# Layer 1 of a two-layer convolution kernel: r and kernel matmuls one product later, the rest of the kernel split in PSUM, VectorE's rest step behind product 8

## What is computed

```python
r = einsum('oc,bchw->bohw', w_reduce, x) + b_reduce
rn = relu(batch_norm(r))
kern = einsum('kc,bchw->bkhw', w_span, rn) + b_span      # 9 values for each pixel
z = softplus(einsum('bkhw,bckhw->bchw', kern, patches))  # 9 shifted copies of x, times kern, summed
y = softplus(conv3x3(z, w_conv2) + b_conv2)
x = x + y
```

## Time and profile before

| | |
|---|---|
| Time, median of 3 runs | 10453.66 us (10447.23 to 10459.92) |
| The profiled execution's own time | 10458.6 us |
| Its span | 10456.8 us |
| Mean granted TensorE clock | 0.971 of full speed |
| PE / DVE / ACT / POOL busy | 91% / 59% / 64% / 47% of the span |
| Layer 1's loop, from about 7619 us | 132 strips, the last product ends at 10443.4 us |

### The profile page before, as it was taken

The page is one execution under the profiler, slowest core; times in us unless marked ns, Lnnn a source line. Parts: engine busy times, 40 slices in busy tenths (PEclk is TensorE's granted clock), DMA queues, the critical chain, the costliest instruction groups (busy, mean ns, idle before and its releaser), DMA issues. The chain is left out here.

```text
span 10456.8 us, 157100 instructions
## 1 busy us (share of the span) xinstructions
PE 9479.5 (91%) x52698; PEld 5411.0 (52%) x52698; DVE 6192.1 (59%) x7749; ACT 6664.2 (64%) x9055; POOL 4891.7 (47%) x2751
## 2 busy tenths in 40 slices
PE   0399999999999999999999999998878888888888
PEld 0266666666666666666666666665222222222222
DVE  4455555555555555555555555555668878888887
ACT  0277676677776776776677777774056666666666
POOL 0233333333333333333333333332067777777777
PEclk9999999999999999999999999999989999999998
DMA  9511111111111111111111111113933333333333
GB/s 195 110 46 45 45 45 45 45 45 45 44 41 42 45 45 45 45 45 45 45 45 45 45 42 40 44 45 80 213 90 95 92 94 94 95 94 92 93 93 95
DMA packets 614703, 715.13 MB, mean 68 GB/s; under 512 B 42861, under 2 KB 576803, under 8 KB 593807
## 3 DMA queue, kind: packets, MB, share of 16 engines
q1 hardware_dynamic: 614670, 714.73, 29.1%
HBM read 549.68 MB, written 164.89 MB: 68 GB/s over the span
## 5 line engine op out<-in xcount | busy, mean ns | idle before, releaser
L507 PE MATMUL banks<-w_hi,hi_lo 128*128 128x256 f16 x18432 | 2351.3, 273 | 53.3 <-DVE hi_lo L731 53.3
L507 PEld LDWEIGHTS banks<-w_hi,hi_lo 128*128 128x128 f16 x18432 | 1784.4, 98 | 458.3 <-ACT qk L622 206.1
L465 POOL TENSOR_TENSOR u_im<-q_im,k_swap 128x512 f32<-128x512 f32 x512 | 701.6, 1370 | 2438.4 <-ACT q_im L640 2402.7
L1161 POOL TENSOR_TENSOR part_sum<-part_sum,prod 128x1024 f32<-128x1024 f32 x660 | 1558.6, 2362 | 53.8 <-DVE prod L1438 1.0
L1196 PE MATMUL banks<-z,conv_w 128*128 128x512 f32 x3136 | 1542.8, 629 | 0.0
L740 DVE TENSOR_TENSOR u<-q_re,banks 128x512 f32<-128x512 f32 x512 | 351.2, 686 | 1893.0 <-ACT q_re L645 1477.4
L622 ACT ACTIVATE qk<-banks,inv_wscale 128x512 f32<-128x512 f32 x1024 | 690.5, 687 | 1069.9 <-PE banks L507 1056.9
L468 POOL TENSOR_TENSOR u<-u,u_im 128x512 f32<-128x512 f32 x512 | 650.6, 1271 | 934.1 <-DVE u L740 934.1
L524 PE MATMUL banks<-hi_lo,w_hi 128*128 128x512 f16 x4608 | 1080.6, 380 | 0.0
L507 PE MATMUL banks<-w_lo_pair,hi_pair 128*128 128x256 f16 x6144 | 1006.1, 273 | 0.0
L455 POOL TENSOR_TENSOR hl_all<-xn,hi_all 64x1280 f16<-64x1280 f32 x258 | 793.9, 3077 | 272.2 <-ACT hi_all L615 260.1
(11 more groups left out here) (191 smaller groups left out, 17316.0 us busy)
## 6 DMA issues: line engine op xcount, KB each, us to landing
xr<-in_x_dram SPq DMA_DIRECT2D x258, 640.0 KB, 8.2
xb<-y_scratch SPq DMA_DIRECT2D x268, 320.0 KB, 4.8
xa<-y_scratch SPq DMA_DIRECT2D x270, 256.0 KB, 5.3
x_res<-in_x_dram SPq DMA_DIRECT2D x258, 256.0 KB, 4.1
out_dram<-res SPq DMA_DIRECT2D x258, 256.0 KB, 5.0
xc<-in_x_dram SPq DMA_DIRECT2D x64, 1024.0 KB, 12.9
y_scratch<-ys SPq DMA_DIRECT2D x256, 256.0 KB, 4.1
yc<-y_scratch SPq DMA_DIRECT2D x256, 256.0 KB, 5.6
```

The costliest lines, as they stand in the source:

```text
L465: nc.gpsimd.tensor_tensor(u_im[:], q_im[:], k_swap[:], ALU.mult).then_inc(u_made, 1)
L507: r = pe.matmul(out, px, w, start=n == 0, stop=n == 13)
L1161: nc.gpsimd.tensor_tensor(part_sum[:], prod[0][:] if n == 0 else part_sum[:], prod[n + 1][:], ALU.add)\
```

## The change

Three things, all in layer 1. On TensorE, the first half of r stands behind select 4 (was 3), the second half behind select 5 (was 4), and the kernel rows behind select 7 (was 6). `k_rest` is no longer a tile of SBUF; it is the columns 256 to 511 of bank 7. Since bank 7 then holds data that `third_parts` still reads, TensorE's waits for `rest_made` become waits for `third_made`, one of them in every strip in front of half 1 of the convolution. On VectorE, `rest` stands behind product 8 (was between 6 and 7), ahead of the sum that follows product 8.

```diff
-            k_rest = tsb("k_rest", [P, 256])
...
+            k_rest = bank[7][:, 256:512]
...
                             select(n, k, 9 * k + n)
                             if n == 1 and any_2:
                                 conv(b, 1, (4, 5))
-                            if n == 3:
+                            if n == 4:
                                 pe.wait_ge(mid_normed, i * 4 + (k + 3))
                                 if any_2:
                                     pe.wait_ge(resid_added[1], i * 4 + (k - 1))
                                 else:
-                                    pe.wait_ge(rest_made, i * 4 + (k + 2))
+                                    pe.wait_ge(third_made, i * 4 + (k + 2))
                                 r_product((k + 2) % 4, 0)
-                            if n == 4:
+                            if n == 5:
                                 pe.wait_ge(rn_ready, i * 8 + (2 * k + 5))
                                 r_product((k + 2) % 4, 1)
-                            if n == 6:
+                            if n == 7:
                                 pe.wait_ge(rn_ready, i * 8 + (2 * k + 6))
                                 weights()
...
                         select(0, (k + 1) % 4, 9 * k + 9)
                         if any_1:
-                            pe.wait_ge(rest_made, i * 4 + (k + 3))
+                            pe.wait_ge(third_made, i * 4 + (k + 3))
                             conv(1 - b, 1, (0, 1))
...
-                            if n == 6:
+                            if n == 8:
                                 rest(i * 4 + (k + 2))
                         v.wait_ge(prod_ready, i * 36 + (9 * k + 9))
                         add_to_x(prod[8])
                         third_parts(i * 4 + (k + 2))
```

More of the change, by code:

```diff
@@ L1244, in _ @@
                     if u:
-                        pe.wait_ge(rest_made, u)
+                        pe.wait_ge(third_made, u)
                     r_product(u, 0)
@@ L1322, in second_parts @@
                     act.wait_ge(rest_made, u + 1)
-                    act.copy(k_parts[:, 1, :], k_rest[:]).then_inc(second_made, 1)
+                    act.copy(k_parts[:, 1, :], k_rest).then_inc(second_made, 1)
                 def conv_abs(v, b, h, ring_used):
@@ L1403, in rest @@
                         v.wait_ge(third_made, u + 0)
-                    v.scalar_tensor_tensor(k_rest[:], b_r[:, 0:256], span_b[:, 0:1], k_parts[:, 0, :], ALU.add, ALU.subtract)\
+                    v.scalar_tensor_tensor(k_rest, b_r[:, 0:256], span_b[:, 0:1], k_parts[:, 0, :], ALU.add, ALU.subtract)\
                         .then_inc(rest_made, 1)
@@ L1408, in third_parts @@
                     v.wait_ge(second_made, u + 1)
-                    v.tensor_tensor(k_parts[:, 2, :], k_rest[:], k_parts[:, 1, :], ALU.subtract).then_inc(third_made, 1)
+                    v.tensor_tensor(k_parts[:, 2, :], k_rest, k_parts[:, 1, :], ALU.subtract).then_inc(third_made, 1)
                 def residual(i, k, age, h):
```

## The result

The changed kernel takes 10287.1 us (median of four, 10281.47 to 10289.03) against 10453.69 for the kernel before: 0.984 of it, 95% interval 0.9823 to 0.9857, or 166.6 us less. The forecast was 10324 with a range from 10288, so the sign was right and the gain came, as forecast, with fewer stretches of TensorE's low clock; the size was not right: 36.9 us more came than forecast, 0.9 us beyond the range.

What follows compares the result with a forecast made beforehand. A waiting loop through several engines set the 21.43 us strip, with TensorE's slow clock adding 1.2 to 1.3. Full-clock 20.2 plus 0.25 gave 20.45: 1.0 us over 130 strips, 130 us less, 10324 against the median; range 10288 to 10460.

Steps and rivals of the forecast that it cites:

- Two loops, P and X: Layer 1: P is TensorE's residual, r, kernel rows and convolution; X is `third_parts`, store, fetches, load of `xb`, `x_up`.
- Select 4 and 5 ahead of r: TensorE, before r: select 4 runs in the 1.85 us idle piece, r undelayed; product 5 ends at 8569.15 instead of 8569.86.
- Kernel rows behind select 7: TensorE, before the convolution: select 7 waits for product 5 either way, so a gain of 0.1 us at most.
- rest behind product 8: VectorE: `rest` adds 0.41 us ahead of the sum and `third_parts`; ScalarE's second part fits beneath the sum.
- k_rest in PSUM: VectorE: `third_parts` becomes constant, taken as 0.48 us, with bounds 0.41 and the mean of about 1.5.
- The new wait: TensorE before convolution half 1 waits for `third_parts`: 0.15 us later than before, giving about 20.2 us a strip.
- ScalarE's later chain: ScalarE behind the later `rest`: residual half 0 and product 0 about 0.95 us later, some 0.7 us of cover remaining.
- Rival 4: ScalarE's later chain binds: perhaps 20.8 us a strip, -80 us, 10374; counted within the forecast's case (0.56).
- The clock: TensorE's shorter idle pieces leave a 1.66 us slow stretch in one strip of six: 20.2 + 0.25 = 20.45 us.
- Rival 1: TensorE's clock falls as often as now: strip 21.25 to 21.45 us, time 10445 (10425 to 10465); chance 0.24.
- rival 3: More slow stretches on TensorE, one of 1.66 us in every strip: 21.86 us, +56 us, 10510; chance 0.10.
- Rival 2: `third_parts` keeps its 1.49 us mean and TensorE waits before convolution half 1: +130 us, 10584; chance 0.10.

Runs made afterwards that it cites:

- PSUM alone: The kernel before with `k_rest` in bank 7 and waits for `third_made` instead of `rest_made`, nothing moved: 10367.5 us.
- filling: The kernel before with four extra selection matmuls ahead of select 3, in TensorE's idle piece before r: 10415.4 us.
- the two runs with `rest` earlier: The changed kernel with `rest` behind product 6 (10271.1 us) or behind product 7 (10264.0 us), all else as changed.
- PSUM with eight matmuls: The kernel before with `k_rest` in PSUM and eight extra selection matmuls ahead of select 3, old order: 10308.7 us.
- the three PSUM kernels with the old order: The kernel before with `k_rest` in PSUM and no, four or eight extra matmuls ahead of select 3: 10367.5, 10335.2, 10308.7 us.
- the order alone: The kernel before with only TensorE's new order (r behind select 4 and 5, kernel rows behind select 7): 10269.6 us.

## Why the prediction was right in its direction and short in its size

- *What bounds the strip.* Two loops, P and X, with slow stretches on the first: right. But the whole excess of 1.25 us over a strip at full clock was put down to the clock. PSUM alone removes 0.74 us of it and leaves 0.63 slow stretches of about 1.3 us; filling takes away nearly half of the stretches and gives 0.24. At 1.3 us for each, the 0.79 stretches of before are 1.0 us; the rest fits loop X with the scattered third part, though no run weighs it by itself.
- *Select 4 and 5 ahead of r.* Right: 1.20, a selection, 0.27 against the walk's 1.2, 0.3, 0.35. Select 4 does not delay r, whose first half starts 0.06 us after the residual's end, as before.
- *Kernel rows behind select 7.* "A gain of 0.1 us at most" compared with the old place in the old order. Against their old place in the new order they lose 0.33 us a strip (19.93 to 19.60). The step lacked this alternative: product 5 comes early enough to need its selection soon, but `rn` is ready earlier still.
- *rest behind product 8.* Priced at 0.41 us ahead of the third part and 0.15 on the strip; measured 0.39 for the instruction (8606.14 to 8606.53), 0.26 for the third part's start, and 0.13 to 0.16 on the strip.
- *k_rest in PSUM.* Taken at 0.48, between 0.41 and 1.5: it was 0.415, at the lower bound, and constant.
- *The new wait.* Expected 0.1 to 0.3 us. The 40.1 us in 107 waits are 0.37 each, but of the weight loads. The matmuls of half 1 start 0.47 us after the selection ahead of them (8607.66 to 8608.13), where convolution products that wait for nothing start 0.32 after theirs, so 0.15 is on the strip; the two runs with `rest` earlier give 0.13 to 0.16. The sum of the walk, 20.08 + 0.15, also counts the 0.07 us of an earlier start twice: with half 1 0.15 us later than in a strip of 20.15, it is 20.3. In the trace half 1 starts 11.75 us behind r's first half, where the walk had 11.91.
- *ScalarE's later chain.* The residual half 0 now waits 186.3 us in 107, 1.7 each, and stays covered: select 2 still ends after product 1, product 2 waits 0.51 us. Rival 4 didn't come.
- *The clock.* This is the step that failed: the term for the slow stretches that are left. The forecast left one in one strip of six, 0.25 us a strip; measured was none in 105 strips. That is 0.25 x 130 = 32 us. The strip itself was 20.09 for 20.2, 14 us. Against them, layer 1's first product starts 9 us later in this trace (7627.8 for 7618.7), in a part that the change hardly touches: the pass before it moved 235 for 242 GB/s, and in the fourteen traces that start lies anywhere from 7618.7 to 7633.3. 32 + 14 - 9 = 37, beside the 36.9 that were missed. That it comes out so well is partly luck: the forecast had also taken off the 4.9 us by which the profiled execution lay over the median, and the end of the changed kernel, behind its last strip, is some 3 us shorter. The range's low end was the case of no slow stretch at all, at the walk's own 20.2, and had no room for the walk's 0.1 us.
- *The reason given for the clock.* It was that "both long idle pieces that now precede slow stretches lose length", the longest being put at 1.95 us. In the waits of 8100 to 10440 us the longest before the kernel rows is 2.4. And length alone does not decide: PSUM with eight matmuls has no piece over 1.1 us and keeps 31 slow stretches, the changed kernel has pieces of 1.2 and 1.1 in every strip and none. The effect was forecast rightly; the ground given for it is not shown.
- *Rivals.* Rival 1 fell by the clock's record; rival 3 by the same. Rival 2 was set aside for the right reason, and the kernel with `k_rest` in SBUF shows what it would have cost beside a steady clock: 0.45 us, 57 us in all, not 130.

Still open: why no slow stretch is left at all. The runs show that work in the piece ahead of r lessens them (0.79 to 0.43, and 0.63 to 0.50 to 0.30), and that the two selections moved ahead of r's halves do more (0.79 to 0.10) than eight added matmuls ahead of select 3; with the kernel rows moved too none is left (0.79 to 0, and 0.63 to 0 with PSUM). Neither the longest idle piece nor the idle time in sum tells them apart: TensorE's listed waits are 2.2 us a strip with eight matmuls and 3.1 in the changed kernel. With eight, all 31 stretches begin while the last matmul started is one of r, so the place of the work may matter. No kernel varied the place alone.

## What to carry to other kernels

Where an engine's in-order queue holds a ready instruction behind a waiting one, swap them even if the ready one isn't on the path: here it took about 0.1 us off a strip at full clock, and with the third part already constant it was worth 0.9% (10367.5 to 10271.1 us), most of it by keeping TensorE's clock. When a strip's length scatters, look at loops that pass near one another: removing one cause may give only the difference to the next loop, so price each with the other removed too. And when three edits come as one, time them apart: the order alone gave at least as much as the whole, and the version with `rest` one product and the kernel rows one selection earlier is 0.6 to 0.7% faster than the change (10221.3 for 10287.1 us; 0.9769 for 0.984).

## What the runs showed of the hardware

- More matmuls made the kernel faster: four redundant ones a strip in an idle piece of 1.85 us took 10463 to 10415 us, eight of them (with `k_rest` in PSUM) 10367 to 10309. One stretch at the low level cost about 1.3 us here, by the three PSUM kernels with the old order.
- The third part, a VectorE instruction of 128x256, takes 0.41 us with both inputs in SBUF if no GpSimd add is running, and otherwise until 0.28 to 0.29 us after that add's end (564 of 564 longer ones, up to 2.59 us). With one input in PSUM it took 0.411 to 0.418 us in all 830 of eight traces, although GpSimd was in an add at the start of 784 of them. The Trainium skill (page SBUF — State Buffer, section Who interferes with whom) states which of the two contends with GpSimd; the times are from these traces. That a change of the strip's rhythm alone, with no operand moved, takes its mean from 1.48 to 0.92 us (the new order alone) is what these runs add.
- The granted clock fell 31 times in 2100 us in a kernel without an idle piece of TensorE over 1.1 us (PSUM and eight matmuls), and never in 105 strips of the changed kernel, which has pieces of 1.2 and 1.1 us in each.
